# Scaled input kept in token order, and read in steps of eight by the input products

## What is computed

```
x = x + conv(ln(x))                        # first half
    # conv: windows of 7 x 7 tokens; w = ln(window)
    #   xB = w @ Bm;  for each of 49 steps: h = xB[step] + h @ A;  xr = h @ Cm
    #   result: xr + gelu(ln(xr) @ W1 + b1) @ W2 + b2
t = x as tokens
t = t + ffn(ln(t))                         # second half
    # ffn: softmax over 4 experts, the best 2 kept and renormalised,
    #   sum over experts of weight * (gelu(ln(t) @ w1 + b1) @ w2 + b2), hidden width 384
```

## Time and profile before

| what | before |
|---|---|
| median of three runs | 1864.97 us |
| the profiled execution's own time | 1863.09 us |
| its span | 1861.4 us |
| mean granted TensorE clock | 0.995 of full |
| TensorE busy | 1809.9 us (97%) |
| VectorE busy | 1527.7 us (82%) |
| ScalarE busy | 1489.4 us (80%) |
| GpSimd busy | 1432.4 us (77%) |

### The profile page before, as it was taken

One profiled execution on the slowest core, in us unless ns is written; L12 is line 12 of the kernel. 1 busy time (PEld: TensorE's weight loads), 2 busy tenths in 40 slices (PEclk: granted clock), 3 DMA queues, 4 the chain that ended last, 5 costly groups with the idle time before them and its releaser, 6 DMA issues.

```text
span 1861.4 us, 35592 instructions
## 1 busy us (share of the span) xinstructions
PE 1809.9 (97%) x8486; PEld 1258.2 (68%) x8486; DVE 1527.7 (82%) x6498; ACT 1489.4 (80%) x2823; POOL 1432.4 (77%) x1097
## 2 busy tenths in 40 slices
PE   5999999999999999999998999999999999999997
PEld 3566665666656666556776777777777777777775
DVE  6899999999999999987886777777777777777775
ACT  1677777777777777778997999999999999999996
POOL 3388888888888888876886878887777777777776
PEclk9999999999999999999998999999999999999999
DMA  6253443344443334335667766666666666666662
GB/s 192 84 166 121 129 125 122 110 122 126 125 125 113 121 121 127 108 124 156 203 208 233 218 214 210 212 213 204 210 210 209 209 205 205 205 205 212 214 209 82
DMA packets 139737, 312.03 MB, mean 168 GB/s; under 512 B 35066, under 2 KB 43925, under 8 KB 139530
## 3 DMA queue, kind: packets, MB, share of 16 engines
q1 hardware_dynamic: 104424, 249.10, 44.5%
q0 software_dynamic: 32000, 58.87, 9.0%
q10 hardware_dynamic: 3106, 1.78, 0.5%
HBM read 243.43 MB, written 67.19 MB: 167 GB/s over the span
## 4 chain that ended last, share of the span: by engine, by line
PE 53%; POOL 23%; issue 13%; DVE 7%; ACT 0%; DVEq 0%; POOLq 0%; ACTq 0%
POOL sorted_rows L522 12%; PE mix_ps L1298 8%; PE mix_ps L1300 8%; PE mix_ps L1299 8%; POOL rstd_xt L511 6%; PE turn_ps L1284 4%; PE up_ps L1284 4%; POOL rstd_r L498 4%; PE turn_ps L1285 4%; PE up_ps L1285 4%; PE turn_ps L1286 4%; PE up_ps L1286 4%; PE tok_ps L1309 4%; PE y_ps L1221 2%; DVE rows L857 1%
## 5 line engine op out<-in xcount | busy, mean ns | idle before, releaser
L570 POOL DMA_INDIRECT out<-out_sb,idx x412 | 430.3, 1045 | 240.8 <-DVE out_sb L1077 127.3
L1036 DVE TENSOR_TENSOR g_lo<-g,g_hi 128x512 fp32r<-128x512 f32 x618 | 423.9, 687 | 194.8 <-ACT g_hi L698 194.4
L522 POOL DMA_INDIRECT sorted_rows<-rows,pos x392 | 452.3, 1154 | 116.7 <-issue 102.4
L698 ACT CAST g_hi<-g 128x512 fp32r<-128x512 f32 x618 | 381.5, 617 | 13.1
L546 POOL TENSOR_TENSOR ex<-euler,rows 128x16 f32<-128x16 f32 x103 | 306.3, 2974 | 0.4
L1173 PE MATMUL y_ps<-g,d_mlp 128*100 128x512 f32 x588 | 292.7, 592 | 0.2 <-ACT g L630 0.2
L1298 PE MATMUL mix_ps<-g_hi,ew 128*96 128x512 f32 x618 | 244.7, 396 | 0.2 <-DVE g_lo L1036 0.2
L1300 PE MATMUL mix_ps<-g_lo,ew 128*96 128x512 f32 x618 | 244.5, 396 | 0.0
L1299 PE MATMUL mix_ps<-g_hi,ew 128*96 128x512 f32 x618 | 243.6, 394 | 0.0
L630 ACT ACTIVATE g<-up_ps 128x512 f32<-128x512 f32 x294 | 170.7, 597 | 64.6 <-PE up_ps L1166 54.6
L692 ACT ACTIVATE g<-up_ps 128x512 f32<-128x512 f32 x308 | 183.7, 597 | 39.8 <-PE up_ps L1286 26.9
(11 more groups left out here) (185 smaller groups left out, 3964.5 us busy)
## 6 DMA issues: line engine op xcount, KB each, us to landing
ew<-expert_w SPq DMA_DIRECT2D x206, 384.0 KB, 4.1
ew<-expert_w SPq DMA_DIRECT2D x206, 288.5 KB, 3.6
rows<-sorted_rows SPq DMA_DIRECT2D x103, 394.0 KB
x_in<-in_x SPq DMA_DIRECT2D x49, 384.0 KB, 3.1
x_raw_t<-in_x_chan SPq DMA_DIRECT2D x49, 384.0 KB, 4.9
rstd_t<-rstd_rows SPq DMA_DIRECT2D x49, 384.0 KB, 4.0
out<-out_sb,idx POOLq DMA_INDIRECT x412
sorted_rows<-rows,pos POOLq DMA_INDIRECT x392
```

Source lines behind the costliest of these rows:

```text
L522: pool.indirect_dma_start(out=sorted_rows[:, :], out_offset=bass.IndirectOffsetOnAxis(ap=pos[:, r, s:s + 1], axis=0), in_=rows[:, r, s, :] ...
L570: pool.indirect_dma_start(out=out_rows, out_offset=bass.IndirectOffsetOnAxis(ap=idx[:, r, s:s + 1], axis=0), in_=out_sb[:, r, s, :], in_of ...
L698: act.copy(g_hi[:, n % PART_RING, :], g[:, n % G_RING, :]).then_inc(hi_done, 1)
L1036: dve.tensor_tensor(g_lo[:, n % PART_RING, :], g[:, n % G_RING, :], f(g_hi[:, n % PART_RING, :]), ALU.subtract).then_inc(lo_done, 1)
```

## The change

The host now lays out `x_chan` in token order (p * 8 + s), the order that `rstd_t` has. `scale_x` multiplies three plain rows. `x_t` is then in token order too, and `from_input` reads it through a view with the sub-tile as outer index: the moving operand of one product is four runs of 128 elements, each in steps of eight elements (32 bytes). Its result lands in the same columns of `mix_ps` as before. Number and size of DMAs, instructions and semaphores are the same.

```diff
-                dve.tensor_tensor(x_t[0:C, :].rearrange("c (s p) -> c s p", s=SUBS), x_raw_t[:, i, :].rearrange("c (s p) -> c s p", s=SUBS),
-                                  rstd_t[:, :].rearrange("c (p s) -> c s p", s=SUBS), ALU.mult).then_inc(x_t_ok, 1)
+                dve.tensor_tensor(x_t[0:C, :], x_raw_t[:, i, :], rstd_t[:, :], ALU.mult).then_inc(x_t_ok, 1)
...
+                by_sub = x_t[:, :].rearrange("c (p s) -> c s p", s=SUBS)
                 for h in range(2):
-                    ins = pe.matmul(mix_ps[0:CG, half(h)], b_aug[:, :], x_t[:, half(h)], start=(r == 0), stop=True)
+                    ins = pe.matmul(mix_ps[0:CG, half(h)], b_aug[:, :], by_sub[:, h * HALF_SUBS:(h + 1) * HALF_SUBS, :],
+                                    start=(r == 0), stop=True)
                 ins.then_inc(h_summed, 1)
...
-        "x_chan": win.reshape(TILES, P, SUBS, C).transpose(0, 3, 2, 1).reshape(TILES, C, TOK),
+        "x_chan": win.reshape(TILES, P, SUBS, C).transpose(0, 3, 1, 2).reshape(TILES, C, TOK),
```

## The result

The changed kernel takes 2008.03 us, median of six runs (2002.24 to 2012.95); the kernel before took 1865.26 beside it (six runs). The ratio is 1.0763, 95% interval 1.0743 to 1.0783: slower by 143 us. The direction was forecast, the time (1962, range 1863 to 1972) was not. The profiled execution took 2005.28 us with a span of 2003.6, 142.2 more than before; the mean granted TensorE clock fell from 0.995 to 0.965.

The account below looks back on a forecast made before the run. The prediction took TensorE, never waiting in stage 1, as the bound: strided input products +97.4 us, first tile +0.35 and -0.81, sum +96.9 on 1863.09, plus 1.9 for the median: 1962 us, 80% range 1863 to 1972, own range 1945 to 1970.

Parts of the forecast that it names:

- Sum: Whole kernel: +97.4 us for input products, +0.35 and -0.81 for the first tile, +96.9 us in all, median 1962 us.
- nothing new opens and nothing absorbs it: TensorE behind `from_input`: it goes straight into `up`, whose input is ready, so the 2 us later end just shifts on.
- the prediction's own lower bound: Input products on TensorE: a strided read just half as fast as plain, 0.86 us per instruction, +83 us over 48 tiles.
- the memory hands over groups of neighbours, one per 1.8 ns, whoever asks: Strided SBUF reads: stride eight leaves one useful element per group, 0.937 us per input product instruction instead of 0.430.
- rival C: TensorE's input products: an isolated element costs what two neighbours do, 0.464 us per instruction, +6.5 us, 1870.7 us; chance 0.06.
- rival D: TensorE's input products: each element fetched twice, 1.87 us per instruction, +277 us, 2141 us; chance 0.03.
- A nanosecond taken off VectorE is worth nothing: Stage 1: TensorE never waits, so 39.8 us less VectorE busy time stays hidden, except -0.81 us at the first tile.
- rival E: Stage 1 period: VectorE's relief reaches it after all, up to -4 us, 1861 us; chance 0.06.
- the scaling's 1218 ns: VectorE's scaling of 1024 elements, all plain: 155 ns fixed plus 1063, 1218 ns instead of 2031.
- hidden layout and loads: Host's layout and load of x by channels: same bytes, same number of transfers, so no effect on time.
- the sign: Whole kernel against before: slower with chance 0.61, same 0.33, faster 0.06.
- Case B: TensorE's input products run as before at 0.43 us, leaving only -0.81 us: 1864.2 us, no change; chance 0.33.

Follow-up runs that it names:

- halves_apart: Changed kernel with TensorE's order altered: state then strided input product of half 0, transposes, then the same for half 1; 1951.20 us, ratio 1.0458.
- dve_only: Kernel before with only VectorE's scaling changed to three plain rows; host layout and TensorE's plain read kept; 1857.44 us, ratio 0.9954.
- r_step8: Kernel before with one of three fp32r products of each `up` reading y_lo in steps of 8, all tiles but the last; 1913.48 us.

## Why the prediction was wrong

1. **The step that failed: "Sum", which left out the clock.** The prediction took the low clock only as a tool to read the earlier trace rows and priced all 48 tiles at full clock. It even wrote that "nothing new opens and nothing absorbs it". TensorE's granted clock fell 12 times in stage 1, 57 us by `halves_apart`. Without them the time would have been some 1951 us, as in `halves_apart`, within the forecast's own range (1945 to 1970; by the terms it names the low end is 1947.5, as 1.9 us for the median were left out). No rival had a clock.

2. **The size of the slow products was right, its reason was not.** Forecast 0.937 us per instruction, measured 0.913; forecast +97 us for the tiles, measured +85, of which VectorE's relief (point 3) has already taken off 6 to 8. As near was the prediction's own lower bound, a read half as fast as the plain one (0.86 us, +83). But "the memory hands over groups of neighbours, one per 1.8 ns, whoever asks" is refuted by `r_step8` (0.82 ns on TensorE). The agreement of 1.83 ns (VectorE's isolated element) with 1.81 ns (four of TensorE's neighbours) was a coincidence, the objection that the prediction raised itself. What fits the numbers is that lower bound, or rival C's price of an element (as two neighbours, 0.464 us forecast) together with rival D's two fetches: C times D gives 0.93 us, and I had them as separate small cases. Which of the two it is stays open. D's counter-argument (plain reads fetched twice would take 0.464, and 0.430 is seen) took the limit seen in fp32r products to hold for reads in fp32, and no row said so.

3. **"A nanosecond taken off VectorE is worth nothing" was wrong**, by 8 us (`dve_only`); rival E (-4 us, chance 0.06) had the direction. The earlier trace rows show no wait of TensorE, because the modelled ends of its products cover the 0.12 us; the row of its weight loads has the wait. GpSimd's loop was the limit, and a scatter of it was held by the scaling. The relief of -4 us at most was half of what it was worth. In the changed kernel it is taken up in the period: 16.44 + 4 x 0.49 = 18.4.

4. **Right:** the scaling's 1218 ns (1221), hidden layout and loads, nothing waiting behind the products, and the sign. Case B (0.430 kept) is excluded.

## What to carry to other kernels

Moving a permuted access to another engine didn't remove its cost here: on the engine without slack each strided instruction was paid in full, and its slower streaming also cost it its clock. So price both, and see whether the slow instructions can stand apart. Before calling an engine the bound, look at each other engine for a loop without a data wait (a share of 80% was one), and at the weight loads' waits beside the products'. A step of 2 in fp32 was nearly free on TensorE, a step of 4 doubled the instruction.

## What was unexpected of the hardware

- An fp32 product of 512 columns takes 0.430 us per instruction plain, 0.453 at step 2, 0.893 at step 4, 0.913 at step 8, 0.853 at step 16; one fp32r product 0.42 instead of 0.235 at step 8.
- VectorE's tensor_tensor of 1024 elements: 1221 ns plain, 2031 with one input in steps of 8, 1963 with the output in steps of 128.
- A GpSimd scatter that starts while VectorE multiplies two SBUF tiles ends 0.96 us after the multiplication does, 2.56 us instead of 0.96 (0.83 us after it where the output is written in steps of 128).
- Twelve falls to 1.2 GHz, about 57 us, with no wait of TensorE's products for another engine between 100 and 880 us; putting the same instructions in another order removed them all.
- A DMA of 1024 pieces of 4 bytes held back the one that waits for it for 11.4 us, 128 pieces of 32 bytes for 3.0.
